# Second attention of a four-layer kernel: probabilities turned by VectorE squares and a DRAM round trip, and a new order of parts

## The chip, the cores and the metric

The kernel runs on one core of a Trainium2 chip as one program. The metric is the device time of one execution in microseconds (us). Before the change, three runs took 2284.98, 2286.3 and 2290.19 us, so the median is 2286.3 us.

## The reference, cut to what matters

x has 16 blocks of 128 tokens with 256 numbers each. Four layers follow one another, and each adds an attention over a context and a feed-forward part to x, so there are eight stages, 0 to 7. The change is in stage 2, the attention of the second layer (16 heads of 128, context of 128 tokens for each block):

```
scores = jnp.einsum('bhtd,bhsd->bhts', q, k) / scale
scores = jnp.where(mask, scores, -jnp.inf)
attn = jax.nn.softmax(scores, axis=-1)
out = jnp.einsum('bhts,bhsd->bhtd', attn, v)
return out.transpose(0, 2, 1, 3).reshape(B, T_text, N_HEADS * HEAD_DIM) @ Wo
```

The product with v sums over the context tokens s. TensorE sums over partitions, while the softmax leaves the query tokens t on the partitions. So the probabilities have to be turned: s onto the partitions.

## The kernel before

**Stages and steps.** Each stage is a list of steps (`STEPS`), done for each of the 16 blocks b and, where a step has several groups, for each group c. Stages 8 and 9 are the routed and the shared experts of the second layer's feed-forward part, stage 3 is its router. Neighbouring stages overlap: block 0 of a stage may start when the stage before has finished that block, and `ROOM` names the stage that must be wholly done first, because its memory is used again (stage 2 needs stage 0 done, stage 3's weights need stage 1 done).

**Order.** The order in which each engine meets its steps is written out ahead of time by a planner: one text for each engine in `ORDER`, one letter for each step, decoded by `letters()` and `timetable()`. Each engine works strictly in that order and waits on semaphores (the `Lane` class). SyncE (SP) has no text; it loads weights, then the router's tiles, then stores, in a loop at the end of `sync_program`.

**Stage 2, one tile.** A tile is block b and group c of four heads, so there are 64 tiles. Steps: `q` (TensorE L1040, 16 matmul records; ScalarE copies it, L1443), `sc` scores (TensorE L1048; VectorE adds the mask bias, L1985, and takes the row maximum, L1988; ScalarE takes the exponentials of four heads, L1448), `pn` (VectorE: reciprocal L1993, normalising L1995), `pt` (TensorE L1054: four transposes of 128x128 into one PSUM bank; ScalarE copies the bank to SBUF, L1455), `pv` (TensorE L1060, probabilities times context; VectorE copies the result, L2000) and `wo` (TensorE L1068, output product; after the fourth group VectorE adds to x, L1683). `P`, `PT` and `OT` have two buffers each. In TensorE's text the steady pattern is `pt`, `q` of the tile two later, `pv`, `sc`, `wo`, and between them stage 3's router steps of an earlier block: `xT` (L844, L845), `r1` (L1081), `pT` (L1086), `acc` (L1090), `rk` (L1095). A block of four tiles is one period of that pattern.

```
elif step == "pt":
    t.wait_ge(S["l1_pn"], nth(b, c, 4))
    p = room(2, "pt", b, c)
    for h in range(4):
        m = eng.transpose(p[:, h * 128:(h + 1) * 128], u.P[i][:, h], ident)
```

**Around it.** SP's `weights(3)` (L735) issues 24 loads of 256 KB once stage 1 is done with its last block (`x_done(1, 15)`). GpSimd takes the reciprocal roots of the layer norms (L2381), scatters the router's rows (L2458, DMA) and stores the experts' tiles (L2474, DMA). After stage 2's last tile come router, table (`tab`), expert weights and the experts' tiles (L1109 on).

## Time and profile before

| what | us |
|---|---|
| median of three runs | 2286.3 |
| lowest and highest run | 2284.98, 2290.19 |
| span of the profiled execution, first to last instruction | 2278.6 |
| median run less that span (what lies around it) | 7.7 |
| TensorE (PE) busy in the span | 2151.6 (94%) |
| VectorE (DVE) busy | 1715.5 (75%) |
| ScalarE (ACT) busy | 1351.4 (59%) |
| GpSimd (POOL) busy | 451.9 (20%) |

The profile gives the profiled execution's span and no time of its own beside it; 7.7 us is the distance of that span to the median run. A busy time is the union of an engine's instructions, so overlapping matmuls count once. PE is the matmul side of TensorE and PEld its weight loads. A float32 matmul shows as two records, a transpose as one. Matmuls are pipelined: the time that one adds is read from the starts of its neighbours, not from its own duration.

### The profile page before, as it was taken

Reading aid. Unit: us, or ns where it says so; the run is one execution under the profiler, and the core shown is the slowest. Engines: PE = TensorE matmul, PEld = TensorE weight load, DVE = VectorE, ACT = ScalarE, POOL = GpSimd, SP = SyncE. Lnnn points to the kernel's source line nnn. Section 1 sums busy time; section 2 is a strip of 40 time slices with the busy share of each in tenths; the row PEclk is TensorE's granted clock in tenths of the full one; section 3 lists DMA queues with packets and bytes.
Section 4 is the critical chain, followed back from the end, with each engine's and each line's share of the span. In section 5 each row is a group of like instructions: output and inputs, shape, how many; then the busy total and the mean of one; then the engine's idle time right before and its main releaser. Section 6 shows DMA issues by size and latency. Waiting matters only on the chain.

```text
span 2278.6 us, 46090 instructions
## 1 busy us (share of the span) xinstructions
PE 2151.6 (94%) x17062; PEld 1683.0 (74%) x17062; DVE 1715.5 (75%) x4847; ACT 1351.4 (59%) x3347; POOL 451.9 (20%) x514
## 2 busy tenths in 40 slices
PE   6899989899999999998999999999899999999998
PEld 4666888888988888887987878885565666665665
DVE  7897999998467777666457887887967767676677
ACT  3677787687744444444643435346677666667662
POOL 3221020000011111021147652003132122212210
PEclk8999999999999999998998999999999999999999
DMA  9300300000020000012211100211000000000000
GB/s 335 105 2 2 117 2 2 2 2 2 23 96 13 11 11 13 13 37 69 89 54 33 52 1 2 99 34 56 1 1 1 5 3 3 5 3 3 3 3 15
DMA packets 53559, 75.29 MB, mean 33 GB/s; under 512 B 4982, under 2 KB 46088, under 8 KB 52440
## 3 DMA queue, kind: packets, MB, share of 16 engines
q1 hardware_dynamic: 48440, 58.96, 7.8%
q0 software_dynamic: 4896, 13.38, 1.8%
q8 instruction: 137, 2.24, 0.4%
q14 instruction: 86, 0.70, 0.1%
HBM read 45.58 MB, written 26.74 MB: 32 GB/s over the span
## 4 chain that ended last, share of the span: by engine, by line
PE 64%; DVE 19%; ACT 10%; issue 4%; POOL 2%; DMA 1%; SPq 0%; POOLq 0%; ACTq 0%; DVEq 0%
PE pb L1040 5%; PE pb L1068 5%; PE pb L917 4%; ACT workA L1589 4%; PE pb L1178 3%; PE pb L1048 3%; PE pb L943 3%; PE pb L1060 2%; PE pb L1250 2%; PE pb L1272 2%; PE pb L1289 2%; PE pb L1273 2%; PE pb L1242 2%; PE pb L1212 2%; PE pb L1012 2%
## 5 line engine op out<-in xcount | busy, mean ns | idle before, releaser
L2381 POOL TENSOR_TENSOR sm<-sm,neghalf 128x1 f32<-128x1 f32 x128 | 74.5, 582 | 858.9 <-DVE sm L1668 858.8
L1448 ACT ACTIVATE workA<-workA 128x128 f32<-128x128 f32 x256 | 99.6, 390 | 162.9 <-DVE workA L1988 162.9
L1421 ACT ACTIVATE areaB<-i128h,workB 128x128 f16<-128x128 f16 x512 | 156.2, 392 | 10.3 <-DVE workB L1941 9.9
L1378 ACT ACTIVATE areaA<-pb 128x512 f32<-128x512 f32 x192 | 105.2, 599 | 57.3 <-PE pb L917 43.0
L917 PE MATMUL pb<-workA 32*128 32x128 f16 (+2 forms) x2048 | 123.3, 257 | 16.1 <-DVE workA L1816 6.4
L917 PEld LDWEIGHTS pb<-workA 32*128 32x128 f16 (+2 forms) x2048 | 92.8, 144 | 52.0 <-issue 29.7
L996 PE MATMUL pb<-areaB 128*128 128x128 f32 x1024 | 125.1, 280 | 0.0
L1040 PE MATMUL pb<-xT,areaA 128*128 128x128 f32 x1024 | 124.7, 275 | 0.0
L1068 PE MATMUL pb<-areaA,workA 128*128 128x256 f32 x512 | 124.2, 386 | 0.2 <-DVE workA L2000 0.2
L1250 PE MATMUL pb<-areaA,workA 128*128 128x256 f32 x512 | 122.7, 383 | 0.2 <-ACT workA L1581 0.2
L1589 ACT ACTIVATE workA<-pb,workA 128x128 f32<-128x128 f32 x256 | 113.9, 460 | 14.4 <-DVE workA L2265 12.7
L996 PEld LDWEIGHTS pb<-areaB 128*128 128x128 f32 x1024 | 120.7, 195 | 0.9 <-issue 0.2
L1040 PEld LDWEIGHTS pb<-xT,areaA 128*128 128x128 f32 x1024 | 119.3, 192 | 0.0
L1596 ACT COPY workA<-pb 128x512 f32<-128x512 f32 x64 | 37.8, 591 | 136.0 <-PE pb L1237 136.0
L1012 PE MATMUL pb<-areaB,workB 128*128 128x256 f32 x512 | 117.2, 388 | 0.0
L2446 POOL TENSOR_TENSOR workA<-workA,neghalf 128x4 f32<-128x4 f32 x64 | 65.4, 1022 | 242.6 <-DVE workA L2243 242.4
L1012 PEld LDWEIGHTS pb<-areaB,workB 128*128 128x128 f32 x512 | 98.6, 195 | 13.1
L1250 PEld LDWEIGHTS pb<-areaA,workA 128*128 128x128 f32 x512 | 93.5, 190 | 19.5 <-issue 6.9
L1068 PEld LDWEIGHTS pb<-areaA,workA 128*128 128x128 f32 x512 | 92.3, 190 | 16.0 <-issue 5.4
L2450 POOL TENSOR_TENSOR workA<-workA,neghalf 128x4 f32<-128x4 f32 x64 | 68.0, 1062 | 176.0 <-DVE workA L2251 176.0
L1231 PEld LDWEIGHTS pb<-workA 128*128 128x128 f32 x512 | 62.8, 192 | 48.9 <-ACT workA L1568 29.9
L2432 POOL TENSOR_TENSOR areaA<-areaA,neghalf 128x32 f32<-128x32 f32 x16 | 88.1, 5512 | 26.9 <-DVE areaA L1784 26.8
(415 smaller groups left out, 5830.4 us busy)
## 6 DMA issues: line engine op xcount, KB each, us to landing
rows_in<-areaB SPq DMA_DIRECT2D x7, 2048.0 KB, 17.5
areaA<-rows_in SPq DMA_DIRECT2D x38, 128.0 KB, 2.0
rows_out<-areaA POOLq DMA_DIRECT2D x38, 128.0 KB, 2.0
areaA<-in_L_xattn_Wo SPq DMA_DIRECT2D x2, 2048.0 KB, 15.8
areaB<-in_edT SPq DMA_DIRECT2D x1, 2048.0 KB, 12.8
areaB<-in_L_ffn_e_up SPq DMA_DIRECT2D x1, 2048.0 KB, 18.2
areaA<-in_wq1T SPq DMA_DIRECT2D x1, 2048.0 KB, 8.3
areaA<-in_L_xattn_Wq SPq DMA_DIRECT2D x1, 2048.0 KB, 9.2
```

Source lines behind the costliest of these rows:

```text
L917: m = eng.matmul(p[i][:, j * 128:(j + 1) * 128], one, two, start=True, stop=True)
L996: m = eng.matmul(p[:, e * 128:(e + 1) * 128], w.ed[:, k, (4 * c + e) * 128:(4 * c + e + 1) * 128], xT[:, k, :], start=(k == 0), stop=(k == 1))
L1012: m = eng.matmul(p[:, 0:256], G[:, e, :], w.eu[:, e, :], start=(e == 0), stop=(e == 15))
L1040: m = eng.matmul(p[:, h * 128:(h + 1) * 128], w.wq[:, 4 * c + h, k], xT[:, k, :], start=(k == 0), stop=(k == 1))
L1068: m = eng.matmul(p[:, 0:256], u.OT[i][:, h], w.wo[:, 4 * c + h], start=(c == 0 and h == 0), stop=(c == 3 and h == 3))
L1250: m = eng.matmul(p[:, 0:256], u.OT[i][:, h], w.wo[:, 4 * c + h], start=(c == 0 and h == 0), stop=(c == 3 and h == 3))
L1378: eng.activation(u.P[n % RP], bank(s, tag, b, c // 2)[:, :], ACT.Exp, scale=1.0 / math.sqrt(hd)).then_inc(freed(s, tag, b, c // 2)[0], 1)
L1421: m = eng.activation(u.far[:, g], i128h[:, :], ACT.Square, bias=u.at[b % 2][:, 8 * c + g:8 * c + g + 1])
L1448: m = eng.activation(u.P[i][:, h], u.P[i][:, h], ACT.Exp, accum_out=u.den[i][:, h:h + 1], bias=u.nm[i][:, h:h + 1])
L1589: m = eng.activation(u.P[i][:, h], p[:, h * 128:(h + 1) * 128], ACT.Exp, accum_out=u.den[i][:, h:h + 1], bias=u.nb[i][:, h:h + 1], scale=u ...
L2381: eng.tensor_tensor(rs, rs, neghalf[:, 0:1], ALU.pow).then_inc(S[f"ln_rs{odd}"], 1)
L2432: eng.tensor_tensor(va, va, neghalf[:, 0:32], ALU.pow).then_inc(S["l2_rs"], 1)
```

## The change

Stage 2's `pt` leaves TensorE and ScalarE. VectorE now transposes each 32x32 square of the four heads where it stands (one instruction of 128x512 into `D`), GpSimd writes `D` to one of four DRAM buffers `turn1` (128 partitions of 2 KB), and SP reads it back with four loads, one for each 32 partitions, in runs of 512 bytes; this puts the squares in their place. `pv` waits for the four loads. Its result now has the queries in another order, which the copy to `OT` undoes; that copy moves from VectorE to ScalarE, which no longer copies the PSUM bank of `pt`. `pv` has two PSUM banks (5 and 6), `PT` has three buffers, `D` two. SP gets an `ORDER` text of its own, in which loads of weights, `pt`, tiles and stores are parts. In it, `small` and `zeros` stand ahead of `weights(1)`, and `weights(3)` stands between the third and the fourth `pt`. VectorE's steps `wo` with c below 3, which do nothing, no longer wait for `ROOM`; `rope` gets a wait on VectorE's own earlier step. All texts of `ORDER` are new, for all stages, with another lettering. The number of parts on each engine is the same but for TensorE (2189 to 2125) and GpSimd (393 to 457); all other work is unchanged.

```diff
@@ STEPS
-        ("pt", 4, "TA"), ("pv", 4, "TV"), ("wo", 4, "TV")),
+        ("pt", 4, "VGS"), ("pv", 4, "TA"), ("wo", 4, "TV")),
@@ ORDER (all texts replaced; the start of SP's)
+    "S": (
+        "badcccecccccccccccccccccccccccccccccccccccccccccccccccccccccccccccccgffffffffffffffffffffffffffffffffffffffhikjjjjjj"
+        "jjjjjjjjjj"),
@@ BANKS
-    (2, "pt"): lambda b, c: (("pt", 5),),
-    (2, "pv"): lambda b, c: (("pv", 6),),
+    (2, "pv"): lambda b, c: (("pv", 5 + c % 2),),
@@ program
+        turn1 = [nc.dram_tensor(f"turn1_{k}", (128, 4, 128), F32).ap() for k in range(4)]
-        u2.PT = [carve(512) for _ in range(2)]
+        u2.PT = [carve(512) for _ in range(3)]
+        u2.D = [carve(512) for _ in range(2)]
@@ sync_program
+            def turned_in(b, c):
+
+                n = 4 * b + c
+                d.wait_ge(S[f"l1_w{n % 2}"], 16 * (n // 2 + 1))
+                if n >= 3:
+                    d.wait_ge(*full(2, "pv", *divmod(n - 3, 4)))
+                src = turn1[n % 4].rearrange("(i r) j w -> i r j w", i=4)
+                for j in range(4):
+                    eng.dma_start(u2.PT[n % 3][32 * j:32 * j + 32].rearrange("r (i w) -> r i w", i=4),
+                                  src[:, :, j, :].rearrange("i r w -> r i w")).then_inc(S[f"l1_r{n % 4}"], 16)
+            for s, step, b, c in order["S"]:
+                if step == "ld":
+                    weights(s)
+                elif step == "small":
+                    small()
+                    zeros()
+                elif step == "in":
+                    tile_in(b)
+                elif step == "pt":
+                    turned_in(b, c)
+                else:
+                    store(b)
@@ tensor_program
-                elif step == "pt":
-                    t.wait_ge(S["l1_pn"], nth(b, c, 4))
-                    p = room(2, "pt", b, c)
-                    for h in range(4):
-                        m = eng.transpose(p[:, h * 128:(h + 1) * 128], u.P[i][:, h], ident)
-                    m.then_inc(full(2, "pt", b, c)[0], 1)
                 elif step == "pv":
-                    t.wait_ge(*freed(2, "pt", b, c))
+                    n = 4 * b + c
+                    t.wait_ge(S[f"l1_r{n % 4}"], 64 * (n // 4 + 1))
@@ scalar_program
-                elif step == "pt":
-                    a.wait_ge(*full(2, "pt", b, c))
+                elif step == "pv":
+                    a.wait_ge(*full(2, "pv", b, c))
                     if two:
-                        a.wait_ge(*full(2, "pv", *two))
-                    eng.copy(u.PT[i], bank(2, "pt", b, c)[:, :]).then_inc(freed(2, "pt", b, c)[0], 1)
+                        a.wait_ge(*wo_gone(2, *two))
+                    eng.copy(u.OT[i].rearrange("p h (i w) -> p h i w", i=4),
+                             bank(2, "pv", b, c)[:, :].rearrange("p (i h w) -> p h i w", i=4, h=4)
+                             ).then_inc(freed(2, "pv", b, c)[0], 1)
@@ vector_program
                 if step == "rope":
                     v.wait_ge(S["cs_done"], 1)
+                    if b:
+                        v.wait_ge(S["l0_y"], b)
@@ (step sc)
                     if two:
-                        v.wait_ge(*full(2, "pt", *two))
+                        v.wait_ge(S["l1_dt"], nth(*two, 4))
-                elif step == "pv":
-                    v.wait_ge(*full(2, "pv", b, c))
-                    if two:
-                        v.wait_ge(*wo_gone(2, *two))
-                    eng.tensor_copy(u.OT[i], bank(2, "pv", b, c)[:, :].rearrange("p (h n) -> p h n", h=4)
-                                    ).then_inc(freed(2, "pv", b, c)[0], 1)
+                elif step == "pt":
+                    n = 4 * b + c
+                    v.wait_ge(S["l1_pn"], nth(b, c, 4))
+                    if n >= 2:
+                        v.wait_ge(S[f"l1_w{n % 2}"], 16 * (n // 2))
+                    eng.transpose(u.D[n % 2].rearrange("p (j h w) -> p h j w", j=4, h=4),
+                                  u.P[i].rearrange("p h (j w) -> p h j w", j=4)).then_inc(S["l1_dt"], 1)
@@ (the loop over ORDER)
-                if s in ROOM:
+                if s in ROOM and (step != "wo" or c == 3):
                     v.wait_ge(*x_done(ROOM[s], NB - 1))
@@ gpsimd_program
-                if step == "cm":
+                if step == "pt":
+                    n = 4 * b + c
+                    g.wait_ge(S["l1_dt"], nth(b, c, 4))
+                    if n >= 4:
+                        g.wait_ge(S[f"l1_r{n % 4}"], 64 * (n // 4))
+                    eng.dma_start(turn1[n % 4], u2.D[n % 2].rearrange("p (j w) -> p j w", j=4)).then_inc(S[f"l1_w{n % 2}"], 16)
+                elif step == "cm":
```

Decoded, TensorE's new text has this piece where stage 1 ends and stage 2's products begin (stage, step, block, group): `1out15 2pv0.0 2sc0.3 2q1.1 2wo0.0 2sc1.0 2pv0.1 2q1.2 2wo0.1 2sc1.1 2sc1.2 2pv0.2 2q1.3 2q2.0 2wo0.2 2pv0.3`. Later pieces look like this: `2pv4.0 2q5.0 2q5.1 2wo3.3 2sc5.0 2sc5.1 2wo4.0 3acc2.0 2pv4.1 2pv4.2`.

## Rows read from the trace of the kernel before

**Rows 1.** The page: busy time of the engines, TensorE's clock in 40 slices.

```profile
PE 2151.6 (94%) x17062; PEld 1683.0 (74%) x17062; DVE 1715.5 (75%) x4847; ACT 1351.4 (59%) x3347; POOL 451.9 (20%) x514
...
PEclk8999999999999999998998999999999999999999
```

**Rows 2.** Busy time by stretch; columns: stretch, PE, PEld, DVE, ACT, POOL, clock, DMA.

```profile
100.00:560.00 460.00, 421.62 (x5075) 368.12 (x5076) 416.09 (x1607) 356.54 (x808) 43.66 (x76) 0.97 0.05 16
...
613.00:1011.00 398.00, 397.67 (x2581) 330.44 (x2580) 278.35 (x830) 183.83 (x674) 44.38 (x57) 1.00 0.08 26
1011.00:1046.00 35.00, 25.21 (x151) 21.00 (x149) 23.02 (x80) 13.87 (x34) 10.18 (x19) 0.83 0.24 65
...
1700.00:2200.00 500.00, 482.67 (x2100) 306.80 (x2099) 343.05 (x744) 337.05 (x788) 105.44 (x113) 1.00 0.01 3
```

**Rows 3.** Timeline of PE in stage 2: start, duration, line; one tile and the next period.

```profile
710.72 0.60 PE L1054 MATMUL pb<-cst,workA 128*128 128x128 f32 x4
711.16 0.27 PE L844 MATMUL pb<-cst,xn 128*128 128x128 f32 x1
...
711.37 1.95 PE L1040 MATMUL pb<-xT,areaA 128*128 128x128 f32 x16
713.16 1.03 PE L1060 MATMUL pb<-workA 128*128 128x512 f32 x2
714.09 1.13 PE L1048 MATMUL pb<-ctxT,workA 128*128 128x128 f32 x8
715.06 1.91 PE L1068 MATMUL pb<-areaA,workA 128*128 128x256 f32 x8
716.80 0.60 PE L1054 MATMUL pb<-cst,workA 128*128 128x128 f32 x4
717.24 1.95 PE L1040 MATMUL pb<-xT,areaA 128*128 128x128 f32 x16
...
736.43 0.27 PE L844 MATMUL pb<-cst,xn 128*128 128x128 f32 x1
```

**Rows 4.** Groups by line: PE's pt, ScalarE's copy of it, VectorE's 128x512 instructions.

```profile
L1054 PE MATMUL pb<-cst,workA 128*128 128x128 f32 x256 | 38.9, 275 | 0.0
...
L1455 ACT COPY workA<-pb 128x512 f32<-128x512 f32 x64 | 36.4, 569 | 6.0 <-PE pb L1054 6.0
...
L1995 DVE TENSOR_TENSOR workA<-workA 128x512 f32<-128x512 f32 x64 | 44.3, 692 | 2.2
...
L2000 DVE COPY workA<-pb 128x512 f32<-128x512 f32 x64 | 43.9, 686 | 42.8 <-PE pb L1060 42.8
```

**Rows 5.** One period by engine (columns as rows 2); VectorE's 128x32 transposes; a 128x16 instruction.

```profile
711.37:736.57 25.20, 25.19 (x167) 20.91 (x166) 18.14 (x55) 11.67 (x44) 3.11 (x4) 1.00 0.03 12
...
L1924 DVE STREAM_TRANSPOSE workB<-workB x48: 168/170/213, 240.6 to 562.0; 128x32 f32<-128x32 f32 x48
...
701.13 0.17 DVE L2053 TENSOR_TENSOR workB<-workB 128x16 f32<-128x16 f32 x1
```

**Rows 6.** Timeline of VectorE and ScalarE, one tile from score to probabilities.

```profile
702.42 0.69 DVE L1985 TENSOR_TENSOR workA<-pb,workA 128x512 f32<-128x512 f32 x1
703.15 0.69 DVE L1988 TENSOR_REDUCE workA<-workA 128x4 f32<-128x512 f32 x1
...
703.87 0.40 ACT L1448 ACTIVATE workA<-workA 128x128 f32<-128x128 f32 x1 [2.96 <-DVE workA L1988]
...
705.33 0.19 ACT L1448 ACTIVATION_READ_ACCUMULATOR workA<-workA 128x1 f32 x1
...
705.78 0.18 DVE L1993 RECIPROCAL workA<-workA 128x4 f32<-128x4 f32 x1
706.00 0.69 DVE L1995 TENSOR_TENSOR workA<-workA 128x512 f32<-128x512 f32 x1
```

**Rows 7.** rows_out: GpSimd's stores (issue ns), landing of its DMAs; SP's 128 KB reads.

```profile
L2474 POOL DMA_DIRECT2D rows_out<-areaA x38: 539/539/789, 1057.3 to 1170.7; - x38
...
DMA to landing us min/median/max: 2.0/2.2/3.8
...
areaA<-rows_in SPq DMA_DIRECT2D x38, 128.0 KB, 2.0
```

**Rows 8.** SP's 24 loads of weights(3), first three and last; landing; packets, 620 to 640 us.

```profile
621.11 0.37 SPq L735 DMA_DIRECT2D areaB<-in_L_ffn_Wup  x1
621.52 0.47 SPq L735 DMA_DIRECT2D areaB<-in_L_ffn_Wgate  x1
622.04 0.47 SPq L735 DMA_DIRECT2D areaB<-in_L_ffn_Wdown  x1
...
636.46 0.67 SPq L735 DMA_DIRECT2D areaB<-in_L_ffn_Wsd  x1
...
areaB<-in_L_ffn_Wsd SPq DMA_DIRECT2D x1, 256.0 KB, 6.9
...
q1 hardware_dynamic: 6133, 5.92, 92.7%
```

**Rows 9.** Timeline where stage 1 ends: its last output product on PE, its add on VectorE.

```profile
613.55 7.07 PE L1012 MATMUL pb<-areaB,workB 128*128 128x256 f32 x32
620.46 1.02 PE L1060 MATMUL pb<-workA 128*128 128x512 f32 x2
...
620.66 0.42 DVE L1683 TENSOR_TENSOR x<-x,pb 128x256 f32<-128x256 f32 x1 [2.30 <-PE pb L1012]
```

**Rows 10.** Timeline of PE at the seam after stage 2: the same products before and behind idle time.

```profile
1030.97 1.16 PE L1152 MATMUL pb<-workB,areaB 128*128 128x128 f32 x8 [0.96 <-ACT workB L1503]
...
1033.96 1.22 PE L1090 MATMUL pb<-bdn,workB 8*128 8x256 f32 x2 [1.73 <-DVE workB L2060]
...
1039.99 1.92 PE L1152 MATMUL pb<-workB,areaB 128*128 128x128 f32 x8
1046.26 0.48 PE L1109 MATMUL pb<-cst,areaA 128*128 128x128 f32 x1 [4.35 <-DMA areaA<-rows_in]
```

More of the change, by code:

```diff
@@ L129 @@
[L129 to L133 removed]
+        "eabeaZbaacabdabdacdddfdbgadhgchhgdhhidhfgdbgdhhhecghdhighdfjghhdkbgidhhegchhhdgihadghjfhdikhbghdehighacgjhdhkhigfdhh"
@@ L232 @@
 LAST_REPEAT = {(2, "out"): 3, (6, "out"): 3}
+ALPHABET = "abcdefghijklmnopqrstuvwxyzABCDEFGHIJKLMNOPQRSTUVWXYZ0123456789+-*/=<>()[]{}!$%&@#^~_:;,.|"
 def letters():
     found = {}
-    for at, (s, steps) in enumerate(STEPS.items()):
-        for k, (step, n, engines) in enumerate(steps + ONCE.get(s, ())):
-            found[s, step] = chr(ord("A" if at % 2 else "a") + k + (12 if s == 9 else 0))
+    for e in "TVAGS":
+        mine = [(s, step) for s, steps in STEPS.items() for step, n, engines in steps + ONCE.get(s, ()) if e in engines]
+        found.update({(e, s, step): ALPHABET[k] for k, (s, step) in enumerate(mine)})
     return found
@@ L261, in timetable @@
                     blocks = 1 if (s, step) in ONCE_STEPS else BLOCKS.get(s, NB)
-                    ahead.setdefault(LETTER[s, step], []).extend((s, step, b, c) for b in range(blocks) for c in range(n))
+                    ahead.setdefault(LETTER[e, s, step], []).extend((s, step, b, c) for b in range(blocks) for c in range(n))
         ahead = {letter: iter(parts) for letter, parts in ahead.items()}
@@ L791, in tile_in @@
             def tile_in(t):
+                if t == 0:
+                    for b in range(NB - 4, NB):
+                        d.wait_ge(*scattered(b))
+                    d.wait_ge(S["m_tab"], 1)
                 if t >= 6:
@@ L795, in tile_in @@
                 eng.dma_start(u8.x[t % 6], rows_in[bass.ds(first_row(t), 128), :]).then_inc(S[f"m_x{t % 6}"], 16)
-            def tiles():
-                for b in range(NB - 4, NB):
-                    d.wait_ge(*scattered(b))
-                d.wait_ge(S["m_tab"], 1)
-                for t in range(TILES):
-                    tile_in(t)
             def zeros():
@@ L810, in zeros, with store @@
                                   bc(zero, 1, [128, n, 256])).then_inc(S["m_zeroed"], 16)
-            for k in range(FIRST + 1, LAST + 1):
-                weights(k)
-                if k == 4:
-                    tiles()
-                if k == 1:
+            def store(b):
+                d.wait_ge(*x_done(LAST, b))
+                eng.dma_start(out[b], x[:, b, :]).then_inc(S["stored"], 16)
+            def turned_in(b, c):
[11 more added lines that the diff above has]
+                elif step == "small":
                     small()
                     zeros()
-            for b in range(NB):
-                d.wait_ge(*x_done(LAST, b))
-                eng.dma_start(out[b], x[:, b, :]).then_inc(S["stored"], 16)
+                elif step == "in":
[4 more added lines that the diff above has]
+                    store(b)
             d.wait_ge(S["stored"], 16 * NB)
```

128 lines of the change are left out of this document (64 added, 64 removed), and 7 rows, old and new, of tables (STEPS, TAKEN).

## The prediction

> **What bounds the kernel now.** I read four views. The page first: TensorE is busy 94% of the span, VectorE 75% [rows 1], so TensorE is the suspect, but a share over eight stages says little about one. Then busy time by stretch: from 613 to 1011 us, where stage 2 runs with the router of stage 3 between, PE is busy 397.67 of 398.00 us at full clock (2.4 GHz), VectorE 278, ScalarE 184, and DMA moves 26 GB/s [rows 2]. Nothing there can be hidden behind PE, and whatever PE is spared there shortens the stretch, as long as nobody keeps it waiting. In the other stages PE idles: 38 of 460 us between 100 and 560, where VectorE is busy 90% of the time, 17 of 500 between 1700 and 2200, and 10 of 35 at the seam behind stage 2 [rows 2]; over the whole span 2278.6 - 2151.6 = 127 us [rows 1]. Third, the timeline: what a step adds on PE is the distance of starts. A `pt` adds 711.16 - 710.72 = 0.44 us, `q` 1.79, `pv` 0.93, `sc` 0.97, `wo` 1.74, and a period of four tiles is 736.43 - 711.16 = 25.27 us [rows 3]. Fourth, groups by line for the other engines [rows 4].
>
> **Part 1, `pt` leaves TensorE.** 64 tiles x 0.44 us [rows 3] = -28.2 us, all of it on the path, since the stretch has no idle time. The group's busy time of 38.9 us [rows 4] would give more, but it counts the overlap with the next step's first matmuls, so I take 0.44. The period becomes 25.27 - 4 x 0.44 = 23.5 us.
>
> **Part 2, VectorE.** It loses the copy L2000 (0.69 us) and gets a transposing instruction of 128x512. The trace has none of that size. Low end: 0.67, as the other 128x512 float32 instructions, all near 0.69 [rows 4]. High end: the 128x32 transposes take 0.17 us [rows 5], and 16 of them would be 2.7. An instruction of 16 columns takes 0.17 as well [rows 5], so that is mostly fixed cost, and I take 0.69: net zero. VectorE is then busy 18.1 us of a 23.5 us period [rows 5], which PE covers. If the cover goes, each 0.1 us more of the transpose is 6.4 us.
>
> **Part 3, ScalarE.** It loses the copy L1455 (0.57 us [rows 4]) and gets one of the same size out of PSUM, with a reordered output. Between 0.57 and, if strides cost, twice that; at 11.7 us busy of a period [rows 5], both ends are covered. Net zero.
>
> **Part 4, the round trip.** From the end of `sc` on PE to `pv`: bias and maximum to 703.87, that is 1.45 us; exponentials 703.87 to 705.52, 1.65; reciprocal and normalising to 706.69, with the hand-over 1.2 [rows 6]; the transpose 0.7; GpSimd's issue 0.54 and landing 2.2 (128 KB; I take it for 256 KB too) [rows 7]; SP's four issues, spaced about 0.5 us as its 256 KB loads are [rows 8], and 2.0 to land [rows 7], 3.5 together. Sum 11.2 us. Ends: 11, and 14.6 if both transfers take the 3.8 us that a DMA on the stores' tensor took at worst [rows 7]. I set this against the PE work that the new text puts between a tile's `sc` and its `pv`, counting the steps between and giving each the time above: at least 12.5 us, median 21.4, and 5 of 64 tiles under 14.6. The rings hold as well: between `pv` n-3, which frees the `PT` buffer, and `pv` n lie 10.6 us or more but for two tiles (5.9 and 7.9), and the four reads need 3.5. So I cost it at 0, with +2 at the far end. Transport: 1 KB packets took 0.927 x 16 x 20 us / 6133 = 48 ns of one DMA engine each [rows 8]. A tile reads 512 runs of 512 bytes, 32 per engine, so at most 1.6 us, and writes 128 runs of 2 KB, 8 per engine, about 0.8: 2.4 us of a 5.9 us tile. SP issues for 2.0 us of each tile and GpSimd for 0.54 beside its two scatters of a block, so neither queue is full. Behind GpSimd's new waits stand the layer norms' roots; its text has them in VectorE's own order, so I cost that at 0, and VectorE's wait on a free `D` too.
>
> The Trainium skill (SBUF — State Buffer, "SBUF: two separate sides" and "A bandwidth-pool intuition that's wrong") warns that a DMA from GpSimd's queue waits for its descriptors while VectorE runs a copy in a two-port mode, and gives 3.1 us in place of 0.62. By it an estimate is a trip 2.5 us longer, with three tiles late, some +2 where the sum has 0. The trace leans the other way: 38 stores beside a working VectorE took 0.54 to 0.79 us to issue [rows 7].
>
> **Part 5, `weights(3)` in SP's text.** It now stands between the reads of tile 0.2 and tile 0.3 and waits for stage 1's last add. Before, that add ended at 621.08 [rows 9], the 24 loads were issued from 621.11 to 637.1, and the last one landed at 636.46 + 6.9 = 643.4, 22.9 us after stage 1's last product left PE at 620.46 [rows 8, 9]. The reads of tile 0.3 queue behind all that: about 24 us after 620.46. PE's text has 19.05 us of work between that product and `pv` 0.3. So PE stalls some 5 us, once (0 to 10: below if the reads slip between weights, above if SP is late from tile 0.2, or if the clock falls behind the gap). The clock: behind the gaps at 1031 to 1038 the same eight records of L1152 took 1.92 us against 1.16 [rows 10], with 0.83 granted in the stretch [rows 2], so a gap can cost more than itself. `zeros` ahead of `weights(1)` costs 0: stage 1's first product is far behind both, after 200 us of PE work.
>
> **Part 6, the new texts elsewhere.** The work is the same; only the 127 us of idle PE can change. I compared, by the same count of PE work between dependent steps, both texts. In stage 6 the distance from `tq` to `sc` grows (median 0.9 to 5.3 us) and from `sc` to `pt` (6.4 to 10.6); stages 0 and 1 are about equal, and there VectorE is nearly full anyway. Behind stage 2 the router of block 14 now falls after the last `wo`, ahead of block 15's, in a chain where PE already idles 10 us [rows 2, 10]: +0 to +6. I take -3 for all of it, between -25 and +25 (a fifth of the idle time lost or added).
>
> **Sum.** 2278.6 - 28.2 + 0 + 5 - 3 = 2252.4 us of span, and 7.7 us around it: 2260. The median of the runs, 2286.3, is that same execution's span plus 7.7, so it is 26 us, or 1.1%, below the median.
>
> **Rivals.**
> (a) The new texts close gaps elsewhere: for it, the longer distances in stages 6 and 7; against it, most of the idle time is in stages 0 and 1. 20 us more: 2240.
> (b) The round trip is partly exposed: if it takes 10 us more, half the tiles come late, since the median distance is 21.4. For it: no row shows a DMA chain of two legs under two queues; against it: the landing times. Half of the gain goes: 2274.
> (c) The slower side: VectorE becomes the bound of stage 2. Its period is 18.1 - 4 x 0.69 + 4t for a transpose of t us. It passes 25.27 at t = 2.5 us, and at 2.7 it is 26.3 us, 1.0 us over, 16 blocks: 2286.3 + 16 = 2302. For it: the 0.17 us for 32 columns; against it: the instruction of 16 columns.
> (d) The new texts lose in stages 0 and 1, where VectorE and PE are both at 90% and a late VectorE step shows at once: 5 to 8% of 460 us more idle, 2283 to 2297.
> (e) The read-back is slow as a transfer, so that stage 2 follows SP's queue. The trace bounds it: it needs 5.9 us per tile against at most 1.6. If runs of 512 bytes took four times the 1 KB packets' 48 ns, a tile would take 6.1 + 0.8 = 6.9 us, 1.0 us x 64 = +64 over the new pace: 2324. The Trainium skill (VectorE: DVE Perf Modes, "The three transpose paths") says so of a plain DMA that transposes by strides, 19 times slower than the crossbar, and leaves VectorE only the squares. Here the squares are turned before the DMA, which moves whole runs of 512 bytes.
>
> **Chances.** Forecast 0.57 (2246 to 2270), (a) 0.12, (b) 0.12, (c) 0.04, (d) 0.13, (e) 0.02. A difference of 0.2%, 4.6 us, is about what a measurement of this kernel can tell from no change. Faster by more: the forecast, (a) and nearly all of (b), 0.80. Within: a part of (b) and half of (d), 0.07. Slower: (c), (e), the rest of (d), 0.13. The range, 2232 to 2288, leaves out (c), (e) and the outer parts of (a) and (d).
>
> **What would show it.** Right: no L1054; stage 2's period near 23.5 us with PE busy throughout; VectorE's transposes near 0.7 us; one gap of some 5 us on PE about 20 us behind stage 1's last product, ended by a DMA into workA. Wrong: a wait of `pv` on a DMA in most tiles (b), VectorE busy over 95% in the stretch and transposes above 2 us (c), PE idle above 50 us between 100 and 560 (d), DMA share above 0.8 in stage 2 (e).

## The result and the profile after

The changed kernel took 2191.12 us (median of 4 runs, 2180.44 to 2193.96), the kernel before in the same job 2285.64 (2281.88 to 2290.19): a ratio of 0.9586 with a 95% interval of 0.9551 to 0.9621. The forecast was 2260 us with a range down to 2232. The sign was right, the size was not: 94.5 us were won, 26 were forecast. The profiled execution took 2190.38 us, its span is 2188.5 us. One of all runs here, among the four of c1 below, took 3519.15 us; the ratios leave it out.

The page after, busy time, TensorE's clock in 40 slices, and the two transfers that are new (they answer to [rows 1]):

```profile
PE 2094.3 (96%) x16806; PEld 1654.5 (76%) x16806; DVE 1695.4 (77%) x4847; ACT 1329.9 (61%) x3335; POOL 484.1 (22%) x578
...
PEclk8999999999999999999996999999999999999999
...
turn<-workA POOLq DMA_DIRECT2D x64, 256.0 KB, 2.4
workA<-turn SPq DMA_DIRECT2D x256, 64.0 KB, 2.0
```

TensorE's (PE's) busy time fell by 57.3 us, twice the 28.2 of the transposes, and its idle time by 32.8 (127.0 to 94.2). To see where, I cut both executions at the same products: the end of stage 1's last output product, of stage 2's, of the last shared expert's, the first query product of stage 6, and the end. Busy time by stretch, before (columns: stretch, its length, PE, PEld, DVE, ACT, POOL, clock, DMA share and GB/s):

```profile
0.00:621.00 621.00, 555.52 (x6612) 475.39 (x6613) 524.12 (x1873) 451.45 (x1015) 70.53 (x129) 0.96 0.16 52
621.00:1016.00 395.00, 394.46 (x2562) 327.08 (x2561) 275.23 (x824) 182.26 (x660) 45.21 (x57) 1.00 0.08 27
1016.00:1201.00 185.00, 170.00 (x1192) 154.99 (x1191) 103.14 (x258) 95.85 (x259) 55.15 (x76) 0.95 0.24 74
1201.00:1539.00 338.00, 330.12 (x3613) 275.03 (x3614) 278.64 (x787) 149.45 (x292) 130.35 (x94) 0.96 0.11 37
1539.00:2276.00 737.00, 701.55 (x3090) 450.48 (x3088) 534.01 (x1108) 472.37 (x1122) 150.69 (x159) 1.00 0.02 8
```

And after:

```profile
0.00:582.00 582.00, 549.69 (x6643) 463.81 (x6644) 514.80 (x1885) 448.48 (x1017) 70.83 (x134) 0.99 0.18 58
582.00:957.00 375.00, 362.54 (x2290) 304.68 (x2288) 263.52 (x807) 180.59 (x663) 78.02 (x114) 0.98 0.36 114
957.00:1145.00 188.00, 170.82 (x1182) 155.70 (x1181) 110.99 (x286) 96.69 (x258) 61.93 (x87) 0.94 0.25 77
1145.00:1488.00 343.00, 326.42 (x3600) 271.65 (x3599) 273.64 (x773) 151.36 (x294) 124.07 (x88) 0.95 0.11 35
1488.00:2186.00 698.00, 684.79 (x3099) 458.65 (x3097) 532.16 (x1100) 452.80 (x1104) 149.22 (x156) 1.00 0.02 8
```

Stages 0 and 1 are 39 us shorter, stage 2 is 20 shorter, stages 6 and 7 are 39 shorter, and the two stretches between, where the experts and stages 4 and 5 run, are 8 longer. Only stage 2 has another kind of work. In stage 2 PE now idles 12.5 us where it idled 0.5. Of these, 12.3 us are three waits of `pv` for the reads of turned tiles, and 9.9 are the first of them. The timeline at that place, SP first, then PE, and the landing of the last load (issue to landing, us):

```profile
580.76 1.73 SPq L827 DMA_DIRECT2D workA<-turn  x4
582.60 0.40 SPq L741 DMA_DIRECT2D areaB<-in_L_ffn_Wup  x1
...
597.34 2.79 SPq L741 DMA_DIRECT2D areaB<-in_L_ffn_Wsd  x1
...
597.80 1.89 PE L1083 MATMUL pb<-areaA,workA 128*128 128x256 f32 x8
609.61 2.93 PE L1075 MATMUL pb<-workA 128*128 128x512 f32 x3 [9.92 <-DMA workA<-turn]
...
areaB<-in_L_ffn_Wsd SPq DMA_DIRECT2D x1, 256.0 KB, 11.2
```

It is the stall that part 5 described: behind the reads of tile 0.2 SP issues the 24 loads of `weights(3)`, and `pv` of tile 0.3 (now L1075) waits for reads that are queued behind them. The other terms of stage 2, VectorE's transposes (L2020) and GpSimd's stores (L2460) with their landing:

```profile
L2020 DVE STREAM_TRANSPOSE workA<-workA x64: 661/711/714, 570.7 to 943.2; 128x512 f32<-128x512 f32 x64
...
L2460 POOL DMA_DIRECT2D turn<-workA x64: 539/573/793, 571.7 to 944.2; - x64
...
DMA to landing us min/median/max: 2.3/2.4/6.8
```

### The profile page after: what moved, and what is told of

Read it like the earlier page. It is cut to its first block, busy times and chain, and to the rows that moved or that the text cites. A ratio compares the mean times of both kernels' runs of the same rounds, so it can differ in the third digit from the quotient of the medians.

```text
span 2188.5 us, 45952 instructions
## 1 busy us (share of the span) xinstructions
PE 2094.3 (96%) x16806; PEld 1654.5 (76%) x16806; DVE 1695.4 (77%) x4847; ACT 1329.9 (61%) x3335; POOL 484.1 (22%) x578
## 4 chain that ended last, share of the span: by engine, by line
PE 66%; DVE 23%; issue 4%; ACT 2%; DMA 2%; SPq 2%; another core or an unknown queue 1%; POOL 0%; DVEq 0%; ACTq 0%; POOLq 0%
PE pb L1060 5%; PE pb L937 4%; PE pb L1083 4%; PE pb L1265 3%; PE pb L1193 3%; PE pb L963 3%; PE pb L1075 2%; PE pb L1068 2%; PE pb L1287 2%; PE pb L1288 2%; PE pb L1220 2%; PE pb L1246 2%; PE pb L1132 2%; PE pb L1221 2%; PE pb L1141 2%
## 5 line engine op out<-in xcount | busy, mean ns | idle before, releaser
L1032 PEld LDWEIGHTS pb<-areaB,workB 128*128 128x128 f32 x512 | 96.1, 190 | 13.5 <-DVE workB L1984 1.1
L2452 POOL TENSOR_TENSOR areaA<-areaA,neghalf 128x32 f32<-128x32 f32 x16 | 87.4, 5469 | 17.5 <-DVE areaA L1803 17.3
L1835 DVE TENSOR_REDUCE workA<-pb 128x4 f16<-128x512 f32 x128 | 83.0, 690 | 8.4 <-PE pb L937 7.9
L963 PE MATMUL pb<-areaA,workA 128*32 128x128 f32 (+1 forms) x1536 | 85.1, 284 | 2.8 <-ACT areaA L1393 2.6
```

The lines of the kernel that those rows point to most:

```text
L963: m = eng.matmul(p[r, k * 128:(k + 1) * 128], vt[:, h, :], P[:, j * 128:(j + 1) * 128], start=True, stop=True)
L1032: m = eng.matmul(p[:, 0:256], G[:, e, :], w.eu[:, e, :], start=(e == 0), stop=(e == 15))
L2452: eng.tensor_tensor(va, va, neghalf[:, 0:32], ALU.pow).then_inc(S["l2_rs"], 1)
```

## The experiments

Theory: the turning gives what the prediction said, and the other 70 us come from the new order of parts in stages whose work did not change. Rival: the turning's freed bank and its move of a copy from VectorE to ScalarE give them, with after-effects. To exchange orders, the texts were cut where a stage's last add stands, at nearly the same progress of the next stage in both kernels, and each engine's text was put together from one kernel's order ahead of the cut and the other's behind it. Jobs ran on different chips. Between the end of stage 2 and stage 6 the same instructions took up to 24 us more on one than on another, and up to 12 us more in one execution than in another on the same chip, so kernels are compared within a job, and by stage in the trace. Elsewhere a stretch with the same order repeats within 2 to 5 us; the changed kernel's stage 2 took 370.9 to 375.6. The labels a1 to e2 stand for the runs in five jobs, a to e.

**First job: each part of the order undone, and the price of the transposes.**

```diff
@@ a1: ORDER, every engine's text
-    up to the end of stage 1: as in the changed kernel
+    up to the end of stage 1: as in the kernel before
@@ a2: ORDER, every engine's text
-    behind the end of stage 5: as in the changed kernel
+    behind the end of stage 5: as in the kernel before
```

> The changed kernel with the order of before for stages 0 and 1 (and of stage 2 what stands among them); everything else as changed. Theory 'the order': the last output product of stage 1 ended at 620.5 us before and at 581.1 after, so 40 us of the gain of 94 come from the order of stages 0 and 1 alone, and this kernel takes 2191 + 40 = 2231 (2220 to 2240). Rival 'the turning': what was won came from the four transposes gone, their bank, and the engine that copies; then the order of stages 0 and 1 is worth less than 5 us, 2191 to 2196. A third reading, that the time is only moved (TensorE late at one seam takes less at the next), gives 2205 to 2215.

> The changed kernel with the order of before from stage 6 on; everything else as changed. Theory 'the order': from the first query product of stage 6 to the last output product of stage 7 the trace has 2275.6 - 1539.5 = 736.1 us before and 2185.5 - 1489.5 = 696.0 after, 40 us for the same matrix work, so this kernel takes 2191 + 40 = 2231 (2220 to 2240). Rival 'the turning': no part of stages 6 and 7 was turned in another way, so if the gain there is an after-effect of stage 2 it stays, 2191 to 2196.

```diff
@@ a3: tensor_program, stage 2, step pv
                     p = room(2, "pv", b, c)
+                    for h in range(4):
+                        eng.transpose(p[:, h * 128:(h + 1) * 128], ident, ident)
@@ a4: sync_program; weights(3) is no longer one piece
                 elif step == "pt":
                     turned_in(b, c)
+                    if 3 <= 4 * b + c < 11:
+                        expert_weights(4 * b + c - 3)
```

> The changed kernel with four transposes of the identity put back on TensorE ahead of each probability-value product, into the bank that the product then overwrites; nothing waits for them. Theory (the price of part 1 of the prediction): 64 times 0.44 us of a TensorE that is busy 98% of stage 2, +28 us, 2219 (2213 to 2224). Rival: TensorE has slack in stage 2 after the change (it gained only 19 us there, of 28), so that they cost 64 times 0.3 or less, under +19 us, 2195 to 2210.

> The changed kernel with the 24 loads of the experts' weights, which SyncE issued in one piece between tiles 0.2 and 0.3, issued three at a time behind the reads of tiles 0.3 to 2.2. Theory: the stall of the probability-value product behind them (9.9 us at 600 us) goes, and nothing else waits for these weights before 976 us, so -9 us, 2182 (2178 to 2186). Rival: VectorE, ScalarE or a buffer is late next at the same place, and only 3 us or less are won, 2188 to 2191.

Measured (medians in us, in brackets the ratio to the kernel before in the same job and its 95% interval), against 2278.51 us for the kernel before: a1 2214.56 (ratio 0.9734, 0.9694 to 0.9774), a2 2207.85 (0.9702, 0.9662 to 0.9741), a3 2186.15 (0.9611, 0.957 to 0.9652), a4 2160.01 (0.9489, 0.945 to 0.9527). The unedited changed kernel was not in this job (its column is its first profile), so I read the stages. The table gives the length of each, between the same products, in us:

| stretch | before | changed | a1 | a2 | a3 | a4 |
|---|---|---|---|---|---|---|
| start to stage 1's last output product | 620.6 | 581.2 | 615.3 | 581.1 | 580.6 | 581.8 |
| from there to stage 2's last | 395.7 | 375.6 | 386.3 | 371.5 | 395.6 | 365.6 |
| from there to stage 6's first query product | 522.4 | 531.7 | 510.4 | 512.8 | 508.7 | 511.4 |
| from there to the end of stage 7 | 737.2 | 697.4 | 697.5 | 738.0 | 695.8 | 697.5 |

The old order gives back 34 us in stages 0 and 1 (a1) and all of the 40 in stages 6 and 7 (a2), each in its own stretch and nowhere else but for 11 to 15 us in a1's stage 2. There TensorE comes to its first output product 16.0 us after stage 1's end for 3.4, so most of this is of the seam at my cut. The four transposes cost 24 us between a2 and a3, 0.38 us a tile where the prediction had 0.44. PE's busy time in the stretch grew by 27 us (361.1 to 388.2, 0.42 us a tile) and its waits shrank by 3. Against the longest stage 2 of that order (375.6) the 24 would be 20, still above the rival's 19. a4 wins 6 to 10 us in stage 2. The third row differs by 19 to 23 us between the changed kernel's profile and these four, though a2 has its very instructions up to stage 6. That is of the chip or the job and not of the edits; all four totals lie below their expected ranges by it and can't be set against 2191.

**Second job: each part of the order done alone, on the kernel before.** The edits are the mirror image (the changed kernel's text ahead of the cut for b1, behind it for b2, both for b3, with stage 2 as before). SP's loop stays as before in them, and all three have the changed waits of VectorE's `wo` and `rope`. b0 is the changed kernel itself.

> The changed kernel once more, unedited, on the chip of the next three. Theory: in its first profile it lost 15 to 23 us between 1050 and 1492 us (granted clock 0.88 where its own copies with later edits show 0.97 to 1.00 for the same instructions), and this is of that execution or chip and not of the kernel; then it stands at 0.951 to 0.955 of the kernel before here. Rival: the loss belongs to the kernel, and it stands at 0.958 to 0.960 again.

> The kernel before, with the changed kernel's order for stages 0 and 1 (and of stage 2 the context products, normalizations and first queries that stand among them); probabilities turned by TensorE as before. Theory 'the order': stage 1's last output product ends 35 to 40 us earlier (620 to 583) and the whole is 34 to 42 us shorter, ratio 0.982 to 0.985. Rival 'together with the turning': the new order of stages 0 and 1 only pays when stage 2 behind it has its bank and VectorE free, under 15 us, ratio over 0.993.

> The kernel before, with the changed kernel's order from stage 6 on. Theory 'the order': from stage 6's first query product to the last output product takes 697 us and not 737, and the whole is 38 to 42 us shorter, ratio 0.981 to 0.984. Rival: under 10 us, ratio over 0.995.

> The kernel before, with the changed kernel's order in stages 0 and 1 and from the end of stage 2 on; only stage 2 is as before, order and turning. Theory 'additive': 36 + 40 us, and 8 for stages 4 and 5, so 80 to 88 us less, ratio 0.961 to 0.965; what is then left to the changed kernel, 20 to 25 us, is all that the turning is worth. Rival 'the parts share a cost': under 65 us, ratio over 0.971.

Measured, against 2283.79 us: b0 2182.41 (0.9562, 0.9515 to 0.9609), b1 2254.23 (0.9861, 0.9816 to 0.9906), b2 2242.61 (0.9808, 0.9763 to 0.9854), b3 2213.29 (0.9685, 0.9637 to 0.9732). The new order alone, with TensorE's transposes still in place, gives 70.5 us, and its two parts give 29.6 + 41.2 = 70.8: they add up, within intervals of some 10 us each. b1 ends stage 1 at 578.8 us, 41.8 earlier than the kernel before. Part of that is lost later, 5 us at the seam that I cut (stage 1's last product to stage 2's first output product, 10.2 us for 4.8), and the rest in the stretch before stage 6, which varies by itself. b2, which has the changed waits of VectorE too, ends stage 1 at 618.6 us for 620.6, and b1 and b3 win theirs with SP's old loop, so neither of these makes the gain of stages 0 and 1. From b3 to b0 30.9 us are left, of which 5.5 are b3's seam: stage 2's turning with its own order is worth some 25 to 31. By the totals b1 (34 to 42 expected) and b3 (80 to 88 expected, under 65 for its rival) fall between theory and rival. By the stages theory holds: b3 has both gains whole, stage 1's end at 578.6 us and 695.6 us in stages 6 and 7. b0 stands between its theory and its rival as well. Its third row is 521.5 us, 10 below the first profile of the same kernel and 9 to 13 above the four runs of the first job.

**Third job: which stage, and is VectorE's new work hidden.**

```diff
@@ c2: ORDER, every engine's text
-    from the end of stage 0 to the end of stage 1: as in the changed kernel
+    from the end of stage 0 to the end of stage 1: as in the kernel before
@@ c3: vector_program, stage 2, step pt
+                    eng.transpose(D, P).then_inc(*v.mark())
+                    v.settle()
                     eng.transpose(D, P).then_inc(S["l1_dt"], 1)
```

> The changed kernel unedited, for a comparison on one chip with the next three, the spread loads above all. Its two profiles have a stop of TensorE of 7.2 and 6.5 us for which no releaser is shown, in the experts' stage (product of the shared expert's gate, at 1114 and 1104 us); four copies with edits elsewhere have none. Theory 'of the program': it is there again, 6 to 8 us. Rival 'of the chip or the moment': it is not there, and the time is 2165 to 2172.

> The spread loads once more, beside the unedited kernel on the same chip. Theory 'two gains': 10 us of stage 2 (stage 1's end to the last output product in 366 us and not 376), and 8 to 15 us in the experts' stage, where the unedited kernel stops at the shared expert's gate and its clock falls; 18 to 25 us less than the unedited kernel. Rival 'one gain': 9 to 11 us less, the remainder having been the other chip's.

> The changed kernel with the order of before for stage 1 alone (from the end of stage 0 to the end of stage 1); stage 0 keeps the new order. Theory 'stage 1': between 100 and 560 us TensorE stood 27.9 us for the expert-product operands that VectorE and ScalarE make, in the kernel before, and 3.3 us in the changed one; that is an order of stage 1, so this edit alone gives back 22 to 36 us. Rival 'stage 0': the longer lead between a block's transpose and its first product (15 us of work more) won it; then this kernel is under 10 us slower than the unedited one.

> The changed kernel with each of VectorE's 64 transposes made twice, one behind the other, into the same tile. Theory 'hidden' (parts 2 and 4 of the prediction): VectorE has 40 us of idle time per 180 in stage 2 and TensorE sets the pace, so 64 times 0.7 us more of VectorE cost within 4 us of nothing. Rival 'VectorE is at its bound there' (rival c in little): 30 to 45 us more.

Measured, against 2281.46 us: c0 2184.9 (0.9576, 0.9539 to 0.9612), c1 2180.93 (0.9546, 0.9501 to 0.9591), c2 2232.71 (0.9779, 0.9743 to 0.9814), c3 2199.41 (0.9643, 0.9605 to 0.9681).

c2 gives back 47.8 us, more than expected: stage 1 ends at 612.5 us for 580.7, and 16 more are lost behind it, where my cut leaves stage 2 less prepared (15.1 us to its first output product for 3.4). So stage 1's order is what matters; the rival of stage 0's lead is out. Where the time goes is seen in the waits of PE between 100 and 560 us (engine, tile and line of the product, what it waited for: us in all, times, longest), before and after:

```profile
PE pb L1005 <- DVE workB L1965: 11.4, 8, 2.1
PE pb L1005 <- DVE areaB L1956: 6.5, 6, 1.4
PE pb L1005 <- ACT workB L1426: 6.4, 4, 2.7
PE pb L1005 <- issue: 3.6, 5, 1.0
```

```profile
PE pb L1025 <- DVE workB L1984: 1.7, 4, 0.8
...
PE pb L1025 <- DVE areaB L1975: 0.7, 2, 0.5
```

L1005 is the product of stage 1 (L1025 after) that hangs on VectorE twice: L1956 builds an operand of it, and L1965 reads an earlier result and so frees its bank. L1426 is ScalarE's operand. Busy time by stretch, before:

```profile
200.00:250.00 50.00, 46.95 (x606) 37.60 (x602) 33.74 (x139) 36.45 (x72) 1.76 (x3) 0.93 0.17 62
250.00:300.00 50.00, 45.83 (x492) 42.85 (x493) 47.63 (x192) 44.60 (x110) 12.71 (x19) 0.97 0.23 73
300.00:500.00 200.00, 179.22 (x1913) 167.03 (x1912) 190.16 (x830) 153.30 (x377) 7.42 (x12) 0.97 0.01 2
```

And after:

```profile
200.00:250.00 50.00, 49.48 (x669) 41.80 (x669) 44.46 (x192) 45.03 (x97) 1.76 (x3) 1.00 0.12 44
250.00:300.00 50.00, 49.62 (x514) 46.14 (x513) 48.56 (x217) 44.20 (x109) 13.90 (x20) 1.00 0.28 91
300.00:500.00 200.00, 197.02 (x2168) 184.58 (x2166) 193.35 (x879) 166.65 (x409) 6.53 (x10) 1.00 0.01 2
```

Before, VectorE was busy 95% from 250 to 500 us and PE waited for it, while it had been busy only 33.7 of 50 us just ahead. The new order does more of stage 1's VectorE work there (44.5 of 50), and both engines then run above 96% beside each other. In c2, with the old order of stage 1 back, VectorE is busy 81.3 us between 200 and 300 us (81.4 before, 93.0 after), and PE waits 21.4 us for it at L1025 again. The earlier start is only a part of the gain, though: VectorE ends this stage's L1965 39.9 us earlier (609.1 to 569.2), and of the idle time that it lost by then (90.7 to 61.9 us), 11 us lie between 200 and 250, 4 between 250 and 500 and 12 behind 500. That the order of stage 1 makes the gain is shown; which feature of it makes how much is read from these windows and not tested. The mean granted clock, 0.93 to 0.97 before, says that PE spent a small part of these stretches at the lower of its two levels (1.2 of 2.4 GHz), where it had waited; after, it is 1.00.

c3 costs 14.5 us, with 20 more in stage 2 (391.2 for 370.9): 64 transposes of 0.71 us are 45 us, and just under half shows, though VectorE is busy 78% of the stretch. The truth lies between 'hidden' and 'bound': a late step of the chain shows before the engine is full. c1 wins 4.0 us, inside the intervals and less than its theory and its rival said; its stage 2 takes 367.3 us for 370.9, with 7.2 us of waits for the reads left. Its expectation of a second gain in the experts' stage fails. In c0 the stop is there again (6.5 us), as its theory said.

**Fourth job: the loads one by one, no trip, and a slower copy.** In d1 `expert_weights(n)` issues one of the 24 loads, where it issued three in a4. Rearrangements are left out of the diff.

```diff
@@ d1: sync_program
                     turned_in(b, c)
+                    if 3 <= 4 * b + c < 27:
+                        expert_weights(4 * b + c - 3)
@@ d2: vector_program, stage 2, step pt; gpsimd and sync: step pt left out
-                    eng.transpose(u.D[n % 2], u.P[i])
+                    eng.transpose((u.PT + u.D)[n % 5], u.P[i])
@@ d3: scalar_program, stage 6, step tq
-                    eng.copy(u.qT[i], bank(6, "tq", b, c)[:, :])
+                    for h in range(4):
+                        m = eng.copy(u.qT[i][:, h], bank(6, "tq", b, c)[:, h * 128:(h + 1) * 128])
```

> The changed kernel unedited, as the measure for the next three on one chip: 0.955 to 0.959 of the kernel before.

> The changed kernel with the 24 loads of the experts' weights issued one behind the reads of each of tiles 0.3 to 6.2 (their first use comes at 932 us). Theory: with three behind each tile the reads of the turned tiles still came late in 3 to 6 tiles (3.7 to 7.2 us); with one (0.7 us of SyncE's time) they don't, and the whole stall of 9.9 us is won: stage 1's end to the last output product of stage 2 in 361 to 364 us and not 371 to 376, 8 to 11 us less than the unedited kernel. Rival: what is late next takes over (TensorE's own work or VectorE), under 5 us less.

> The changed kernel without the round trip: GpSimd's store and SyncE's four reads are left out, VectorE turns the squares straight into one of five tiles, and the probability-value product reads that (so the 32x32 squares stand in the wrong places, and the output of the second attention is another). Theory 'hidden' (part 4 of the prediction): apart from the stall behind the weights' loads, which goes with it (9.9 us, as the product no longer waits for SyncE), the trip costs nothing: 8 to 14 us less than the unedited kernel. Rival 'partly exposed' (rival b): 20 us or more less.

> The changed kernel with ScalarE's copy of the turned queries of stage 6 made in four pieces of 128 columns in place of one of 512, so each of the 64 takes some 0.4 to 0.5 us longer (28 us of ScalarE in all). The new order has 5.3 us of other TensorE work between the transposes of the queries and the scores that need them (median), where the old had 0.9. Theory 'distance': here it is hidden, under 6 us more. Rival: it is not the distance but the sum of ScalarE's work that counts, 15 us or more, as in the kernel before with the same edit (run next, where the theory expects 18 to 30 us more).

Measured, against 2284.36 us: d0 2188.77 (0.9592, 0.954 to 0.9644), d1 2175.83 (0.9533, 0.9497 to 0.9569), d2 2170.3 (0.9513, 0.9473 to 0.9554), d3 2189.53 (0.9594, 0.9557 to 0.9631). d1 is 13 us faster than the changed kernel by the medians, 8.5 of them in stage 2 (364.2 us for 372.7, and below all six profiles of the changed order there); the others lie in the stretch before stage 6, which varies by itself. What is left of the stall in d1, the waits of PE in stage 2:

```profile
PE pb L1085 <- DMA workA<-turn: 2.8, 2, 1.8
```

d1 is the version that is better than both kernels, though its interval and d0's overlap. d2, without the trip, is 5.5 us faster still, 5.0 of it in stage 2 (359.2 us): that is all the trip costs, and 2.8 of it are the waits that d1 has left. Against the unedited kernel d2 wins 13.5 us in stage 2, as 'hidden' said (8 to 14), and 18.5 by the medians, under the rival's 20. d3 costs 0.8 us, as 'distance' said.

**Fifth job: why the old order loses 40 us in stages 6 and 7.** e2 is d3's edit on the kernel before.

```diff
@@ e1: scalar_program, stage 7, step gu
-                                   ACT.Silu).then_inc(freed(7, "gate", b, c)[0], 1)
+                                   ACT.Exp).then_inc(freed(7, "gate", b, c)[0], 1)
```

> The kernel before with the exponential in place of SiLU in stage 7 (so the hidden values of the last feed-forward are others; the amount of work is the same). ScalarE then keeps one table for the softmax of stage 6 and for stage 7: of its 63 table loads of 1.28 us, 49 stand in stages 6 and 7, and they go (the new order has 31 there). Theory 'tables': what the new order won in stages 6 and 7 came through the 18 loads that it saves; then without any the old order is as good as the new, stages 6 and 7 take under 705 us and not 737, and the whole is 30 to 45 us less (ratio 0.980 to 0.987). Rival 'distance': the loads lie beside TensorE's work and the old order loses by products that follow too closely on the copies they need; under 12 us less (ratio over 0.995).

> The kernel before with the same edit as on the changed kernel: ScalarE's copy of the turned queries of stage 6 in four pieces, some 28 us of ScalarE more in all. On the changed kernel it cost 0.8 us. Theory 'distance' (and also 'ScalarE is late', by tables or by order): here it shows, 18 to 30 us more (ratio 1.008 to 1.013). Rival: the old order hides it as the new one does, under 6 us more (ratio under 1.003).

Measured, against 2280.6 us: e1 2282.16 (0.9986, 0.9958 to 1.0014), e2 2292.9 (1.0037, 1.001 to 1.0064). e1's stages 6 and 7:

```profile
1546.00:2280.00 734.00, 701.95 (x3091) 451.00 (x3090) 534.50 (x1110) 409.41 (x1073) 150.70 (x159) 1.00 0.02 8
```

63 us of ScalarE's work are gone (472.4 to 409.4), and the stretch is 3.6 us shorter: the table loads were almost all hidden, that theory falls. e2's edit was smaller than I had put down. The copies of the turned queries by group, in the kernel before and in d3 (in windows of 400 us):

```profile
L1568 ACT COPY workA<-pb 128x512 f32<-128x512 f32 x36 | 21.7, 602 | 0.0
```

```profile
L1586 ACT COPY workA<-pb 128x128 f32<-128x128 f32 x156 | 30.8, 300 | 14.9 <-PE pb L1233 14.9
```

Four pieces are busy 30.8 / 39 = 0.79 us for 0.60, so some 12 us of ScalarE over 64 tiles and not 28. In the old order it lengthened stages 6 and 7 by 8.1 us (737.2 to 745.3), in the new one by 0.6 (697.2 to 697.8). So the old order shows ScalarE's latency and the new one hides it. That is of the kind that 'distance' says, and e2 falls short of its numbers only as the edit does. In the old order PE has many short waits between 1539 and 2276 us. The longest in total are those of the scores (L1231) for the exponentials of an earlier tile, of the transposes (L1237) for the normalising, of `pv` (L1242) for the copy of the turned probabilities, and of `q` (L1205) for ScalarE's squares:

```profile
PE pb L1231 <- ACT workA L1589: 7.0, 12, 0.6
PE pb L1237 <- DVE workA L2272: 6.1, 4, 3.5
PE pb L1242 <- ACT workA L1596: 5.4, 13, 0.7
PE pb L1205 <- ACT workA L1558: 3.0, 11, 0.3
```

After, those on ScalarE have all but gone (0.7 us for the scores, now L1246, and 0.1 idle in all before `pv`, now L1257); one of 3.3 us stays before the transposes (now L1252). The copy of the turned queries is not in this list. It is in the list of TensorE's weight loads (PEld), which wait where PE still counts as busy with the matmuls before. The weight loads of the scores, waiting for that copy, in the kernel before, in e2 and in the changed kernel:

```profile
PEld pb L1231 <- ACT workA L1568: 29.9, 46, 0.8
```

```profile
PEld pb L1231 <- ACT workA L1569: 38.7, 46, 1.0
```

```profile
PEld pb L1246 <- ACT workA L1585: 1.7, 4, 0.5
```

That is the distance from `tq` to the scores: in the old order the copy was late for 46 of 64 tiles, by some 0.65 us each, and in the new one for 4. e2 adds 8.8 us to this wait and 8.1 to the stretch, d3 adds 1.2 (2.9 us, 6 times) and 0.6; a2, with the old order back, has 30.0 us, and b2, with the new order on the kernel before, 1.7. Part of each wait lies beside the matmul before it, so 28 us is an upper bound of what this distance won of the 40. All waits of weight loads for ScalarE and VectorE in these two stages sum to 81.2 us before and 35.9 after. No run moved single products alone, so the shares are not tested.

## Why the prediction was wrong

**Bound.** PE sets the pace in stage 2: right. Putting work on it (a3) costs 24 us of a priced 28, putting 45 us on VectorE (c3) costs 20.

**Part 1**, -28.2. Right. a3 measures 24 with the new order; d1, whose stall is nearly gone, has a stage 2 that is 395.7 - 364.2 = 31.5 us shorter than before. That is more than the transposes' price, so stage 2's own new order has a part in it; no run separates the two.

**Parts 2 and 3**, transpose at 0.69 us, net zero. The transpose takes 0.711 us, so the 128x16 row [rows 5] was the right one to go by. The cover is thinner than I wrote: c3 lets 45% of an added transpose through.

**Part 4**, the trip at 0 to +2. Nearly right: 5.0 us between d1 and d2. GpSimd's issue took 0.573 us and landing 2.4 (I had 0.54 and 2.2), SP's four issues 1.73 and landing 2.0 (2.0 and 2.0) [rows 7, 8]. The far end, 3.8 us for a landing, was too near: the store issued at 593.15 us, in the middle of the weights, landed after 6.8. Rivals (b), (c) and (e) did not come about; the DMA share of stage 2 is 0.36. (The period of rival (c) at 2.7 us is 15.3 + 4 x 2.7 = 26.1 us and not 26.3, so its time was 2300.) The Trainium skill's warning (SBUF — State Buffer, "SBUF: two separate sides") of GpSimd's descriptors waiting for VectorE would, as an estimate from its figures, have made the trip 2.5 us longer. The trace does not show it: of the 64 stores under a VectorE that is busy 70% of the time, the 32 whose landing is recorded took 2.4 us (median), against 2.2 for the stores of before [rows 7]. But VectorE's 128x512 instructions there are additions, products, reductions and transposes and none is the copy that the warning speaks of, so this case is hardly a test of it.

**Part 5**, a stall of 5 us, once. Right in place and kind, 9.9 in size, the upper end of 0 to 10. I had let the reads land 24 us behind the moment when stage 1's last product leaves PE. They landed 28.6 us behind it (581.05 to 609.61): the first load was issued 1.55 us after that moment where it had been 0.65, the 24 issues took 17.5 us for 16.0, and the last load landed 11.2 us after its issue for 6.9, at 608.55 us [rows 8, 9]. The four reads, issued from 600.66 us on, were there 1.1 us later. So the term that I mis-sized here is the landing of the loads, which I took over from the kernel before.

**Part 6**, the new texts elsewhere, -3 between -25 and +25. **This is the step that failed.** It measured -70.5 by b3, or -70 by the stretches of the two profiles (-39.4, +3.2, +6.1, -39.8). Two errors lie in it. First, "only the 127 us of idle PE can change" took all busy time for work. In stages 6 and 7 the same products have 701.6 us of busy time before and 684.8 after, next to 35.4 and 13.2 us of idle: over 40% of that gain came out of what the page calls busy. Weight loads waited there for copies just made while PE's earlier matmuls still counted as busy (29.9 us before the scores alone). In stages 0 and 1 another 5.8 us of busy time went as the granted clock rose from 0.96 to 0.99. Second, I judged the order by distances in PE's text alone. In stage 6 that gave the right mechanism (`tq` to `sc`, 0.9 to 5.3 us), and I priced it at next to nothing, -3 us with all the others. In stage 1 it could not see the cause at all: there "VectorE is nearly full anyway" was true of the average, 90% [rows 2], and false of the 50 us ahead of its full stretch. An engine that is full from 250 us on and two thirds busy from 200 to 250 can be started earlier; b1 (the order of stages 0 and 1) and c2 (of stage 1) show that the whole order is worth 30 to 48 us by the medians and 32 to 42 at stage 1's end. The slack ahead is 11 us of it; what makes the rest stays open.

**Rivals.** (a) had the right mechanism at 20 us; it should have been allowed 50 to 75, and then the range, which ended at 2232, would have reached the result. (d) went the other way.

**Sum.** Span 2278.6 - 39.4 - 20.1 + 3.2 + 6.1 - 39.8 = 2188.6, measured 2188.5. These are the differences of the stretches and must add up. The forecast priced the second alone (-28.2 + 5 = -23.2) and gave the other four -3 together. That the second came out so near is in part luck: PE's busy time in the stretch fell by 32 us (395.2 to 363.1) and not 28, and its waits grew by 12 (0.5 to 12.5) and not 5.

## What to carry to other kernels

A new order of parts is a change of its own, even where it comes with another: price it by stage, and don't bound its gain by the idle time of the busiest engine: busy time can hold waits, and for TensorE they show at its weight loads. Ask of each engine that waits whom it waits for, cut that engine's busy time into short windows, and look for slack just ahead of the stretch where it is full, but check how much of the gain that slack can carry. When a load queue gets work with a deadline, put bulk loads between its items one at a time, as far ahead as their first use allows: here it came 331 us after the last of them had landed (608.55 to 939.43 us).

## What the runs showed of the hardware

A wait of TensorE can hide in its busy time: in the old order the weight loads of stage 6's scores stood 29.9 us for ScalarE's copy, and the list of PE's waits between 1539 and 2276 us has none for it.

In the experts' stage PE stops once at the shared expert's gate, in every kernel with the new order there and on every chip but one. No releaser is shown, but for d3, where it is ScalarE's L1520. The timeline of the changed kernel:

```profile
1112.74 1.95 PE L1159 MATMUL pb<-workB,areaB 128*128 128x128 f32 x16
...
1121.91 1.43 PE L1167 MATMUL pb<-workB,areaB 128*128 128x128 f32 x5 [7.22 <-issue]
```

It was 6.5 us in b0, 6.2 in b3, 6.5 in c0, 7.3 in c1 and c2, 3.2 in c3, 7.1 in d0, 6.5 in d1, 3.2 in d2 and 8.6 in d3. It was absent in a1 to a4, which all ran on one chip, and in b1, b2, e1 and e2, which have the old order there. With the waits behind it, PE idled 18 to 28 us between the first expert tile and stage 5's first product, where those had 9 to 13. ScalarE stood at the same time (6.15 us, put down to an unknown releaser). So it goes with this order, and with the chip or the job; what it is stays open, and no run was made for it. It explains a part of why a4 took 2160 us in one job and c1, the same kernel, 2181 in another: of the 18.9 us between their profiles before stage 6, 4 lie before the end of the shared experts and 15 behind it, where c1 idled 13.9 us for 3.8 and the granted clock was 0.95 for 0.97.

The transposes of c3 were another surprise: an engine that is idle 22% of a stretch still passed on 45% of what was added to it.
